# Expert stage: two row pairs as 25 tiles, in regions of 13 and 12

## The reference, cut to what matters

```python
x = x + conv_sweeps(ln_c(x))
t = to_tokens(x)                                  # (16, 3600, 64)
n = ln_t(t)
p = softmax(n @ router_w + router_b)              # 8 experts
top_p, top_i = top_k(p, 2); top_p /= top_p.sum()
out = einsum('bnd,edc->bnec', n, expert_w) + expert_b
t = t + sum over the 2 chosen of top_p * out[top_i]
```

## Time and profile before

| | us |
|---|---|
| median of 3 runs | 1315.49 |
| lowest and highest | 1314.47, 1316.27 |
| profiled execution, its own time | 1316.26 |
| its span, first to last instruction | 1314.2 |
| first expert matmul at | 906.80 |

### The profile page before, as it was taken

The page is one execution under the profiler, slowest core; times in us unless marked ns, Lnnn a source line. Parts: engine busy times, 40 slices in busy tenths (PEclk is TensorE's granted clock), DMA queues, the critical chain, the costliest instruction groups (busy, mean ns, idle before and its releaser), DMA issues.

```text
span 1314.2 us, 32957 instructions
## 1 busy us (share of the span) xinstructions
PE 1277.7 (97%) x11240; PEld 1168.7 (89%) x11240; DVE 758.8 (58%) x1646; ACT 546.9 (42%) x1477; POOL 548.4 (42%) x684
## 2 busy tenths in 40 slices
PE   7999999999998999999999999996999999999997
PEld 5999999999998999999999999995777777777776
DVE  4666665555555222222222222226999999999996
ACT  5455555343334222222200000006767676776763
POOL 1455554000000000000044444445888888888886
PEclk9999999999999999999999999998999999999999
DMA  4122222000000000000011211110010100101011
GB/s 158 53 70 73 64 67 82 0 0 0 0 0 0 0 0 0 0 0 0 0 45 67 67 67 49 64 45 1 27 52 26 51 27 29 48 26 52 26 52 51
DMA packets 15529, 47.44 MB, mean 36 GB/s; under 512 B 2928, under 2 KB 3184, under 8 KB 15472
## 3 DMA queue, kind: packets, MB, share of 16 engines
q1 hardware_dynamic: 15328, 46.28, 10.2%
q10 hardware_dynamic: 144, 0.33, 0.1%
HBM read 31.86 MB, written 14.75 MB: 35 GB/s over the span
## 4 chain that ended last, share of the span: by engine, by line
PE 95%; DVE 2%; ACT 1%; issue 1%; POOL 1%; DMA 0%; DVEq 0%; ACTq 0%; POOLq 0%
PE twin L1046 35%; PE twin L957 28%; PE twin L1108 14%; PE twin L1122 7%; PE twin L1073 6%; PE twin L1089 3%; PE twin L996 2%; PE twin L977 0%; PE twin L984 0%; DMA x_in<-x 0%; DVE tnum L682 0%; DVE act_buf L895 0%; DVE scratch L886 0%; ACT x_in L557 0%; ACT scratch L593 0%
## 5 line engine op out<-in xcount | busy, mean ns | idle before, releaser
L1046 PE MATMUL twin<-kbuf,late 128*128 128x136 f32 (+2 forms) x3940 | 457.8, 280 | 5.0 <-DVE kbuf L797 5.0
L1046 PEld LDWEIGHTS twin<-kbuf,late 128*128 128x128 f32 x3940 | 457.6, 192 | 5.3 <-DVE kbuf L797 5.3
L957 PE MATMUL twin<-parts 128*128 128x384 f32 (+2 forms) x2070 | 380.9, 343 | 3.7 <-DVE act_buf L668 2.2
L957 PEld LDWEIGHTS twin<-parts 128*128 128x128 f32 x2070 | 368.4, 189 | 6.9 <-DVE act_buf L668 2.9
L325 POOL TENSOR_TENSOR act_buf<-kbuf,x_in 128x144 f32 (+1 forms) x198 | 96.8, 489 | 562.5 <-DVE kbuf L803 562.5
L803 DVE SCALAR_TENSOR_TENSOR kbuf<-twin,act_buf 128x144 f32<-128x144 f32 x394 | 121.3, 308 | 336.8 <-PE twin L1046 336.8
L1108 PE MATMUL twin<-em,parts 64*128 64x512 f32 x1404 | 224.4, 424 | 8.5 <-ACT x_in L557 7.5
L556 ACT ACTIVATE x_in<-twin 128x384 f32<-128x384 f32 (+1 forms) x90 | 40.4, 448 | 262.1 <-PE twin L1073 259.9
L1108 PEld LDWEIGHTS twin<-em,parts 64*128 64x128 f32 x1404 | 116.7, 188 | 33.2 <-ACT x_in L557 7.7
L542 ACT ACTIVATE act_buf<-kbuf 128x144 f32 x196 | 63.2, 323 | 167.1 <-DVE kbuf L803 167.1
L695 DVE SCALAR_TENSOR_TENSOR act_buf<-twin,act_buf 128x400 f32 (+1 forms) x70 | 40.2, 575 | 75.6 <-PE twin L957 52.1
(11 more groups left out here) (118 smaller groups left out, 1552.1 us busy)
## 6 DMA issues: line engine op xcount, KB each, us to landing
x_in<-x_col SPq DMA_DIRECT2D x20, 720.0 KB, 4.1
result<-act_buf SPq DMA_DIRECT2D x36, 400.0 KB, 2.9
scratch<-x_tok SPq DMA_DIRECT2D x8, 448.0 KB, 3.3
spare<-x_tok SPq DMA_DIRECT2D x8, 448.0 KB, 3.3
scratch<-x_tok SPq DMA_DIRECT2D x8, 384.0 KB, 3.1
spare<-x_tok SPq DMA_DIRECT2D x8, 384.0 KB, 3.1
x_in<-x SPq DMA_DIRECT2D x3, 400.0 KB, 5.2
x_in<-x SPq DMA_DIRECT2D x2, 200.0 KB, 4.1
```

Source lines behind the costliest of these rows:

```text
L957: last = mm(acc[:, lo:hi], vw[:, k, wpart, si], carry[:, cpart, g, lo + s * BG:hi + s * BG], start=first and si == 0, stop=final and si == ...
L1046: last = mm(banks[CONV[g]][:, lo * BG:hi * BG], hw[:, k, si], kbuf[:, g, lo + s:hi + s].rearrange("p j b -> p (j b)"), start=si == 0, stop ...
```

## The change

Two row pairs (3200 columns, 25 whole tiles) are taken together, as one region of 13 tiles and one of 12. There are still 18 regions, but 225 tiles instead of 234. A region is named `r` = (i, s), with s from 0 to 3, so that i counts four regions or 50 tiles; `tile_no`, `chunk_no`, `back_no`, `group_no` and `region_no` give the running numbers that the semaphore waits need. The short region has four chunks instead of five and three groups of additions instead of four. No tile repeats columns, so `tile_lo` and the addition of the tail are gone; the 13th tile of a long region crosses from the first row pair into the second. The result bank and the gated buffer follow the running tile number. The looping engines go three times over four regions. Each table of orders has two entries, for long and short regions. SyncE stores both row pairs of a pair of regions, the first once the long region's four groups are added.

```diff
-        ACT_TILES = (4, 6)
-        COPY_TILES = (0, 1, 2, 5, 10, 11, 12)
+        ACT_TILES = [(4, 6), (4, 6)]
+        COPY_TILES = [(0, 1, 2, 5, 10, 11, 12), (0, 1, 2, 5, 10, 11)]
         TERMS = [(0, 0), (0, 1), (1, 0)]
         LAG = 3
-        SEQ = 2 * TILES
         QUAD = 4
-        GROUPS = -(-TILES // QUAD)
-
-        def act_gates(j, p):
-
-            tiles = ACT_TILES + COPY_TILES
-            return len(tiles) * j + sum(a <= p for a in tiles)
+        BC = 3
+        PAIR_TILES = 2 * REG // TN
+        NT = [-(-PAIR_TILES // 2), PAIR_TILES // 2]
+        NCH, NBK, NGR = ([-(-t // size) for t in NT] for size in (TC, BC, QUAD))
+        SEQ = 2 * PAIR_TILES
+
+        def count_of(per, r):
+
+            i, s = r
+            return i * (2 * sum(per)) + (sum(per) * (s // 2) + per[0] * (s % 2))
+
+        def tile_no(r):
+            return count_of(NT, r)
+
+        def chunk_no(r):
+            return count_of(NCH, r)
+
+        def back_no(r):
+            return count_of(NBK, r)
+
+        def group_no(r):
+            return count_of(NGR, r)
+
+        def region_no(r):
+            return count_of([1, 1], r)
+
+        def behind(r):
+            i, s = r
+            return (i, s - 1) if s > 0 else (i - 1, 3)
+
...
+        def place_of(s, p):
+            return PAIR_TILES * (s // 2) + NT[0] * (s % 2) + p
         def stage_of(k):
             k = k % SEQ
-            return k if k < 6 else (k - 6) % 5
-
-        def stage(slot, p):
-
-            return gated[stage_of(TILES * slot + p)]
-
-        def stage_age(slot, p):
-
-            k = TILES * slot + p
+            return k % 6 if k < 30 else (k - 30) % 5
+        def stage(s, p):
+            return gated[stage_of(place_of(s, p))]
+        def stage_age(s, p):
+            k = place_of(s, p)
             return next(d for d in range(1, SEQ + 1) if stage_of(k - d) == stage_of(k))
...
+        def tokens_of(r):
+
+            i, s = r
+            at = s % 2 * NT[0] * TN
+            return act_buf[:, :].rearrange("p (k n) -> p k n", n=2 * REG)[:, i * 2 + s // 2, at:at + NT[s % 2] * TN]
...
-        TURN_AT = [(7, 1), (8, 1), (9, 1), (11, 0), (12, 2)]
-        COPY_AT = [(7, 0), (7, 1), (10, 0), (11, 0), (12, 0)]
-        VAR_AT = [(7, 2), (9, 0), (9, 2), (11, 0), (12, 2)]
-        INV_AT = [(8, 0), (8, 1), (11, 0), (11, 1), (12, 1)]
-        SCALE_AT = [(8, 1), (10, 0), (10, 0), (12, 1), (12, 1)]
-        BACK_AT = [(1, 2), (2, 2), (4, 0), (5, 1), (6, 1)]
-        HIGH_AT = [(1, 1), (2, 0), (3, 0), (4, 1), (5, 1)]
-        LOW_AT = [(1, 2), (3, 0), (3, 2), (5, 2), (6, 1)]
-        STEP_AT = [(2, 0), (2, 2), (3, 0), (3, 1), (4, 1), (5, 2), (6, 1), (7, 2), (8, 2), (9, 0), (9, 2), (10, 2), (10, 2), (11, 1), (12, 1), (12, 2), (12, 2)]
-        EXP_AT = (7, 1)
+        TURN_AT = [[(7, 1), (8, 1), (9, 1), (10, 2), (12, 1)],
+                   [(7, 1), (8, 1), (9, 1), (10, 2)]]
+        COPY_AT = [[(7, 1), (8, 0), (9, 1), (11, 0), (11, 1)],
+                   [(7, 0), (8, 0), (10, 0), (11, 0)]]
+        VAR_AT = [[(8, 1), (8, 2), (9, 2), (11, 2), (12, 2)],
+                   [(8, 0), (8, 2), (9, 2), (11, 0)]]
+        INV_AT = [[(9, 1), (9, 1), (10, 0), (12, 1), (12, 1)],
+                   [(8, 0), (8, 1), (11, 1), (11, 1)]]
+        SCALE_AT = [[(9, 0), (9, 1), (10, 1), (12, 1), (12, 1)],
+                   [(9, 0), (11, 0), (11, 1), (11, 1)]]
+        BACK_AT = [[(0, 2), (2, 2), (3, 2), (5, 1)],
+                   [(1, 2), (3, 0), (3, 2), (5, 1), (6, 1)]]
+        HIGH_AT = [[(1, 0), (2, 0), (4, 0), (5, 0)],
+                   [(1, 0), (3, 0), (3, 0), (5, 0), (5, 1)]]
+        LOW_AT = [[(1, 1), (3, 0), (3, 2), (5, 2)],
+                   [(2, 0), (3, 0), (4, 0), (5, 1), (6, 1)]]
+        STEP_AT = [[(2, 2), (3, 1), (4, 0), (4, 2), (5, 1), (6, 0), (7, 0), (8, 0), (8, 1), (9, 1), (10, 0), (11, 0), (11, 0), (11, 1), (11, 2), (12, 1), (12, 2)],
+                   [(2, 1), (2, 2), (3, 0), (3, 2), (4, 0), (4, 2), (5, 2), (6, 1), (6, 2), (8, 0), (9, 0), (9, 1), (9, 2), (10, 2), (11, 0), (11, 2), (11, 2)]]
+        EXP_AT = [(11, 0), (7, 1)]
...
 
-            def store(j):
-                sp.wait_ge(s_o, 2 + GROUPS * (j + 1))
+            def store(k, q):
+                sp.wait_ge(s_o, k * sum(NGR) + (2 + NGR[0] + NGR[1] * q))
                 for g in range(G):
-                    sp.dma_start(out[j, :, g], cols[:, j, g]).then_inc(s_out, 16)
-
-            with sp.Fori(0, HP) as j:
-                store(j)
+                    sp.dma_start(out[k * 2 + q, :, g], cols[:, k * 2 + q, g]).then_inc(s_out, 16)
+
...
-                if later(j):
-                    act.wait_ge(s_tb, n - NCK + 1)
+                if not first_region(r):
+                    last = min(TC * c + k, NT[1 - s % 2]) - 1
+                    act.wait_ge(s_tb, back_no(behind(r)) + last // BC + 1)
...
+            def add_out(r, g):
+
+                i, s = r
+                lo, hi = g * QUAD, min((g + 1) * QUAD, NT[s % 2])
+                dve.wait_ge(s_y, tile_no(r) + hi)
+                dst = tokens_of(r)[:, lo * TN:hi * TN].rearrange("p (t r n) -> p r t n", r=2, n=C)
+                src = twin[SUMS[0] // 2][:, :, 0:(hi - lo) * C].rearrange("p r (t n) -> p r t n", n=C)
+                nc.vector.tensor_tensor(dst, src, dst, ALU.add).then_inc(s_o, 1)
+
...
+            region((0, 0), (0, 1), (0, 2))
+            with pool.Fori(0, 3) as i:
+                for s in range(1, 5):
+                    region(*((i + (s + d) // 4, (s + d) % 4) for d in range(3)))
+            for s in range(1, 4):
+                region((3, s), (3 + (s + 1) // 4, (s + 1) % 4), (3 + (s + 2) // 4, (s + 2) % 4))
+            region((4, 0), (4, 1), None)
+            region((4, 1), None, None)
 
...
-            def tile_lo(p):
-                return min(p * TN, REG - TN)
...
+            def channels(r, c, bank=CTB):
+
+                i, s = r
+                back = back_of(c, s)
+                pe.wait_ge(s_xn2, chunk_no(r) + back[-1] // TC + 1)
+                if first_region(r):
                     if c >= 2:
                         pe.wait_ge(s_tl, c - 1)
                 elif c == 0:
-                    pe.wait_ge(s_cp, NCK * (j + 1))
+                    pe.wait_ge(s_cp, chunk_no(r) + NCH[s % 2])
                 else:
-                    pe.wait_ge(s_tl, n)
-                for i, p in enumerate(tiles_of(c)):
-                    last = mm(banks[bank][:, TN * i:TN * (i + 1)], tl[:, c, i, 0:P], ident[:, :],
+                    pe.wait_ge(s_tl, back_no(r) + c)
+                for k, p in enumerate(back):
+                    last = mm(banks[bank][:, TN * k:TN * (k + 1)], tl[:, p // TC, p % TC, 0:P], ident[:, :],
                               start=True, stop=True, is_transpose=True)
...
+                if p % BC == 0:
+                    pe.wait_ge(s_tl, back_no(r) + p // BC + 1)
+                if tile_no(r) + p >= 2:
+                    pe.wait_ge(s_g, tile_no(r) + p - 1)
+                    old, at_old = (r, p - 2) if p >= 2 else (behind(r), NT[1 - s % 2] + p - 2)
+                    if at_old in ACT_TILES[old[1] % 2] + COPY_TILES[old[1] % 2]:
+                        pe.wait_ge(s_ga, act_gates(old, at_old))
...
```

More of the change, by code:

```diff
@@ L592, in gate_odd, with region @@
                 for e in range(E):
-                    last = act.activation(stage(slot, p)[:, e, C:P], twin[(TILES * slot + p) % 2][:, 1, e * C:(e + 1) * C],
-                                          ACT.Copy, scale=gate[slot][:, 2 * p + 1, e:e + 1])
+                    last = act.activation(stage(s, p)[:, e, C:P], result(s, p)[:, 1, e * C:(e + 1) * C],
+                                          ACT.Copy, scale=gate[s % 2][:, 2 * p + 1, e:e + 1])
                 last.then_inc(s_ga, 1)
-            def region(j, slot, now, front):
-                for p in range(TILES):
+            def region(r, now, front):
+                q = r[1] % 2
+                for p in range(NT[q]):
@@ L621, in _ @@
[L621 to L632, removed]
@@ L633, in _ @@
-            region(HP - 2, 0, HP - 1, None)
-            region(HP - 1, 1, None, None)
+                            for c in at(INV_AT[q], p, place):
+                                inv_std_tokens(front, c)
+                            for c in at(COPY_AT[q], p, place):
+                                copy_tokens(front, c)
+            for c in range(NCH[0] + 2):
+                if c < NCH[0]:
+                    copy_tokens((0, 0), c, FILL_CT[0][c])
+                if 1 <= c <= NCH[0]:
+                    inv_std_tokens((0, 0), c - 1)
+                if 2 <= c < NBK[0] + 2:
+                    first_part((0, 0), c - 2, FILL_TB[c - 2])
@@ new lines, in _ @@
+            copy_tokens((0, 1), 0, FILL_CT[1][0])
+            copy_tokens((0, 1), 1, FILL_CT[1][1])
+            exponential((0, 0))
+            for c in range(NCH[1]):
+                inv_std_tokens((0, 1), c)
+                if c + 2 < NCH[1]:
```

(64 more changed lines are left out.)

359 lines of the change are left out of this document (159 added, 200 removed).

## The result

The changed kernel takes 1303.95 us, median of 4 runs (1303.79 to 1304.12), against 1315.88 for the kernel before (four runs; the median of the three ahead was 1315.49): ratio 0.9911, 95% interval 0.9895 to 0.9927. That is 11.9 us faster. The forecast was 1298.7; the time is inside the range given (1295.5 to 1304.5), outside the 1297 to 1301.5 of the likeliest case. The profiled execution took 1304.02 us for a span of 1302.2.

The account below looks back on a forecast made before the run. TensorE's issue was taken to bound the expert stage. Terms 11.25 + 3.5 + 2.3 + 0.77 - 0.12 - 0.9 = 16.8 us saved gave 1299.5 profiled, 1298.7 as median; range 1295.5 to 1304.5.

Parts of the forecast that it names:

- the likeliest case: Whole kernel: the forecast itself, 1298.7 us, with its own range from 0 to 0.3 us a pair and two tile prices; chance 76%.
- the signs set beforehand: Expert stage: prediction wrong if a pair of regions takes over 44 us or the span shrinks by less than 12.
- The loops: VectorE, ScalarE and GpSimd looping over four regions instead of two: no cost from instruction fetches; other end 5.8 us, or 17.
- Rival 2: Looping engines: the four-region loop fetches code at every way back, 5.8 us, so 1304.5, far end 1316; chance 6%.
- The removed work: TensorE, nine short regions: 13th tile's matmuls and sums 11.25 us, one-tile chunks turned to tokens 3.5, turned back 2.3.
- VectorE's reserve: VectorE's first gate after a short region: about 0.2 of 0.7 us reserve stays; cost 0.1 us a pair, 0.9 in all.
- Rival 1: Short regions: VectorE becomes the bound, 0.6 to 0.8 us a pair, 1303 to 1305; chance 9%.
- The start: TensorE's wait before its first expert tile: ends 0.77 us earlier, as region 1's fifth chunk is gone.
- The end: Last region's final result addition: ends 1.13 us earlier, 0.12 less than the 1.25 counted for the tile.
- Rivals 3 and 5: TensorE: 3, new tables remove waits, 1294 to 1296.5, 5%; 5, gates fall behind the following block, 25 us, 1324, 3%.
- rival 4: Removed tile: worth only an average one, 1.74 us, 15.7 in all, 1300.6; inside the forecast's own range, no separate chance.

## Why the prediction was right or wrong

The sign and the order of size were right, and the reading that TensorE's issue is the price of everything held: in the undisturbed regions 1 to 15 it is busy throughout. By the signs set beforehand it is a near thing: a pair takes 42.81 us, under the 44, but the span shrank by 12.0 where less than 12 was to mean wrong.

**The step that failed** is "The loops": "I take nothing for one of four". The runs put 8.4 us in its place. The other end given there was a fetch at each of two ways back at 2.9 us, 5.8 in all; the stand itself is of that size (2.6 to 3.2 over all runs), but what it costs TensorE was not priced: holes of 1.7 to 2.4 us, and behind most of them the low clock, 2.1 to 5.2 us lost per way back. Rival 2 was the mechanism that acted, on top of a forecast that was otherwise too low in gain. I called its chance 6% although VectorE's and ScalarE's bodies nearly doubled; that the old loops fetch nothing told only of bodies of 196 and 183 entries. The Trainium skill, "Runtime: NRT & Kernel Launch", section "Instruction fetch mechanics", says that a taken branch to code outside the two blocks held waits for a fetch; that stood against the change and was right in kind: the traces show such waits, 2.6 to 3.2 us long. That the outcome depends on the place, as such blocks would have it, the moved loops agree with. Its block size none of the runs settles.

**Luck.** The time lies in the range because two errors pull against each other. With 8.4 us lost and the other terms as forecast the gain would have been 16.8 - 8.4 = 8.4 us, and the time, about 1307.5 us, outside.

**The removed work was under-priced.** Sums of start-to-start distances on TensorE, a pair before (two times region 9) and after (regions 7 and 8):

```
                    before        after        less   predicted
expert blocks       26, 21.68     25, 20.67    1.01   0.78
16-transpose sums   14,  7.46     13,  6.88    0.58   0.47
8-transpose sums    12,  3.40     12,  3.28    0.12   0
one-tile chunks      4,  1.40      2,  0.70    0.70   0.70
```

A block costs more where the next is of another kind (an expert block 0.88 before a chunk, about 0.8 before a sum; a long sum 0.59 before a chunk, 0.47 to 0.49 before experts), and I had priced the tile by its cheap neighbours: 0.46 us a pair too little. By regions, a short one saves 1.67 us (forecast 1.69) and a long one 0.73 (0.26). That split misleads: the removed tile's long sum had stood three tiles later, in the long region, and an 8-transpose sum moved there from the short one, so the pair is what to compare. A part is not the tile's at all: the kernel before written out takes 45.0 a pair, so 0.2 of the 0.46 is what its loops cost under the old table.

**VectorE's reserve** (0.1 us a pair) came out at nothing; the place I named, the first gate after a short region, is where the old table's loss of 0.7 begins, inside the 0 to 0.8 I had bounded. The new table puts those steps earlier: the last begins 1.4 us after region 8's start instead of 2.1. Rival 1 is thus real with the old order, and did not act. The start: from the last one-tile turn back to the first expert tile 899.09 to 906.42 is 7.33 us, before (898.70 to 906.80) 8.10: 0.77, as said. The first region after it, though, takes 23.0 us as before. The end: last region to last addition 20.0 us against 21.3, 1.3 for 1.13. Rivals 3 and 5 did not show (TensorE idles 1.7 us in region 16, 1.8 before); rival 4 is refuted, a pair saving 2.4 and not 1.74. Its 1300.6 was also counted from the profiled time; from the median it is 1299.8.

Together, by the starts of the regions: regions 1 to 15 take 339.0 us before and 329.2 after, 320.8 without the 8.4, so 18.2 less where my terms give 15.3. The first region gives nothing (0.3), the last two 1.9 (1.4), the start in the span 0.4 (0.8; it moves by half a microsecond and more from run to run). That is 20.5, less 8.4 is the 12.0 of the spans.

## What to carry to other kernels

When a loop's body grows, count what each engine issues per pass and look at the first entries behind the branch and at the instruction queue's packets just there (its total says less: 40 where two engines stood, 21 with VectorE written out and ScalarE's loop moved to where it didn't stand, 25 to 28 written out); if they stand, write the loop out or move it. Do it for every engine: one that stands is enough. A short stand on a side engine is dear where TensorE is full, because the clock may fall behind the hole. Price a removed block by the distances of the blocks around it, not by the one at hand.

## What the runs showed of the hardware

Way back of a loop: bodies of 114 to 242 entries of the trace never stood; one of 326 stood 2.6 to 3.2 us or not at all, by its place in the program; one of 359 did not; bodies of 360 and 383 stood 2.8 to 3.0.

Behind holes of 1.7 to 2.1 us TensorE's clock stayed at a mean of 1.00 over three regions (2.1 to 2.5 us lost) and fell to 0.93 or 0.88 in the nine others, whose holes were 1.8 to 2.4 (3.3 to 5.2 us lost); the length of the hole does not separate them, and what does is open.

Loops of two regions that don't stand cost some 0.1 us a region under the old table, loops of four under the new tables nothing that the traces show.
